# Attention chain on one core: head 0's k stack in halves, V projections between the scores, third reciprocal six steps earlier

## What is computed

```python
xn = group_norm(x) * gn_gamma + gn_beta
q, k, v = xn @ wq.T + bq, xn @ wk.T + bk, xn @ wv.T + bv     # 8 heads of 32
scores = einsum('bhqd,bhkd->bhqk', q * scale, k)
attn = softmax(scores, axis=-1)
o = einsum('bhqk,bhkd->bhqd', attn, v)
out = o @ wo.T + bo + residual
```

## Time and profile before

| what | value |
|---|---|
| median of 3 runs | 504.64 us (504.47 to 504.94) |
| the profiled execution's own time | 505.75 us |
| its span, first to last instruction | 504.0 us |
| mean granted TensorE clock | 0.971 of 2.4 GHz |
| busy: TensorE, weight loads | 474.6 us (94%), 241.0 us (48%) |
| busy: VectorE, ScalarE, GpSimd | 360.9 (72%), 270.2 (54%), 209.2 (42%) |

### The profile page before, as it was taken

The page is one execution under the profiler, slowest core; times in us unless marked ns, Lnnn a source line. Parts: engine busy times, 40 slices in busy tenths (PEclk is TensorE's granted clock), DMA queues, the critical chain, the costliest instruction groups (busy, mean ns, idle before and its releaser), DMA issues.

```text
span 504.0 us, 7046 instructions
## 1 busy us (share of the span) xinstructions
PE 474.6 (94%) x2252; PEld 241.0 (48%) x2252; DVE 360.9 (72%) x684; ACT 270.2 (54%) x518; POOL 209.2 (42%) x195
## 2 busy tenths in 40 slices
PE   8899999998999998999999999998899999999996
PEld 6454444443338664544444432664444444433363
DVE  6699888884853557987677747629798677748573
ACT  3238777776603323786667663131687566756032
POOL 8200021137010001799898951000589798990100
PEclk9979999999896998999999999999899999999999
DMA  5330432104100053387973541034257975352002
GB/s 148 59 59 17 139 66 36 21 13 85 23 12 1 13 128 89 66 193 153 183 174 67 99 91 23 1 87 109 66 113 155 185 149 101 58 98 48 17 2 83
DMA packets 19984, 40.69 MB, mean 81 GB/s; under 512 B 7282, under 2 KB 8442, under 8 KB 19820
## 3 DMA queue, kind: packets, MB, share of 16 engines
q1 hardware_dynamic: 14652, 24.23, 20.5%
q0 software_dynamic: 5152, 16.00, 17.2%
q10 hardware_dynamic: 144, 0.02, 0.0%
...
## 4 chain that ended last, share of the span: by engine, by line
PE 62%; issue 12%; DVE 7%; POOL 5%; SPq 4%; DMA 4%; ACT 4%; POOLq 0%; ACTq 0%; DVEq 0%
PE S L932 16%; PE S L959 12%; PE PV L970 10%; DVE max L696 5%; DMA k_stack<-kL 4%; PE S L1084 3%; PE PV L887 3%; POOL SUMS L489 3%; ACT E L552 3%; SPq L308 2%; PE M L913 2%; PE S L913 2%; PE PV L913 2%; PE S L1129 2%; SPq L315 1%
## 5 line engine op out<-in xcount | busy, mean ns | idle before, releaser
L696 DVE TENSOR_REDUCE max<-S 128x1 f32<-128x512 f32 x384 | 238.8, 674 | 19.2 <-PE S L932 18.8
L552 ACT ACTIVATE E<-S 128x512 f32<-128x512 f32 x384 | 211.9, 605 | 63.0 <-PE S L959 54.2
L489 POOL TENSOR_TENSOR SUMS<-E 128x512 f32<-128x512 f32 x120 | 158.2, 1437 | 125.4 <-ACT E L552 125.0
L932 PE MATMUL S<-k_stack,q_stack 126*128 126x512 f32 x384 | 181.2, 482 | 6.5 <-DVE max L696 3.2
L959 PE MATMUL S<-q_stack,k_stack 128*128 128x512 f32 x384 | 156.6, 420 | 9.1 <-ACT E L552 8.5
L932 PEld LDWEIGHTS S<-k_stack,q_stack 126*128 126x128 f32 x384 | 73.7, 192 | 82.4 <-DVE max L696 59.8
L959 PEld LDWEIGHTS S<-q_stack,k_stack 128*128 128x128 f32 x384 | 73.8, 194 | 38.5 <-ACT E L552 24.1
L970 PE MATMUL PV<-E,V 128*32 128x512 f32 x768 | 91.7, 598 | 0.0
L709 DVE TENSOR_TENSOR mHL<-S,mHL 4x128 fp32r<-4x128 f32 x48 | 13.3, 277 | 51.9 <-ACT mHL L541 51.9
L970 PEld LDWEIGHTS PV<-E,V 128*32 128x32 f32 x768 | 20.6, 109 | 46.6 <-issue 26.8
L468 POOL TENSOR_TENSOR att<-pv_sb,rec_sb 128x512 f32<-128x512 f32 x9 | 12.3, 1371 | 70.5 <-DMA rec_sb<-den_sb 70.5
(11 more groups left out here) (176 smaller groups left out, 339.2 us busy)
## 6 DMA issues: line engine op xcount, KB each, us to landing
...
k_stack<-kH SPq DMA_DIRECT2D x32, 128.0 KB, 2.4
q_stack<-qH SPq DMA_DIRECT2D x40, 64.0 KB, 2.0
...
k_stack<-kL SPq DMA_DIRECT2D x16, 128.0 KB, 3.7
q_stack<-qH SPq DMA_DIRECT2D x16, 128.0 KB, 2.3
q_stack<-mHL SPq DMA_DIRECT2D x96, 2.0 KB
q_stack<-qL SPq DMA_DIRECT2D x20, 64.0 KB, 2.0
```

The costliest lines, as they stand in the source:

```text
L489: pool.tensor_tensor(SUMS[:, slot, :], E[:, E_PLAN[s][0], :], E[:, E_PLAN[s + 1][0], :], ALU.add).then_inc(sum_ready, 1)
L552: act.activation(E[:, slot, :], B[:, ring_of_scores(s) % B_RING, :], ACT.Exp, scale=1.0 if l == 0 else float(HEAD_DIM[l]) ** -0.5).then_in ...
L696: dve.tensor_reduce(max8[:, m % 2, r:r + 1], A[:, n % A_RING, :], AX.X, ALU.max, negate=True).then_inc(a_used, 1)
L932: pe.matmul(A[:, n % A_RING, :], q_stack[0:SHIFT_ROW, slot, q0:q0 + P], k_stack[0:SHIFT_ROW, slot, k0:k0 + HALF], start=True, stop=True).t ...
```

## The change

Head 0's k stack is loaded in two halves of its columns, the first counting on `stack_dma[0]` and the second on a new semaphore, `half_dma`; the high parts of q and k are sent once ScalarE has written them, the low parts after the subtraction. The maxima of unit 0 take the first half of k for all four tiles of queries, then the second; the fifth score waits for `half_dma`. In layers 2 and 3 four projections instead of seven run ahead of the scores, the V projections between them at steps -15 to -1, and projections 8 to 11 at steps 1 to 15, with their copies and subtractions moved accordingly; ScalarE copies the last two V projections after the first rows of maxima. In all layers the third reciprocal moves from step 123 to 117, and GpSimd's normalisation waits for `pv_out` too.

```diff
--- before.py
+++ after.py
@@ -43,7 +43,7 @@
 RES = 16
 W_COLS = (3 * 128 + C, 4 * C, 4 * C)
 FOLDED = BLOCKS - 1
-REC_STEPS = (66, 94, 123)
+REC_STEPS = (66, 94, 117)
 PER_ROW = HALF // DP
 LEAD_GROWTH = (1, 3, 5, 7)
 VALUE_STEPS = ((29, 37, 45, 53), (61, 69, 77, 85), (93, 101, 107, 115))
@@ -189,6 +189,7 @@
         xn_ready = sem("xn_ready")
         proj_done, v_out, high_ready, split_ready = sem("proj_done"), sem("v_out"), sem("high_ready"), sem("split_ready")
         stack_dma = [sem(f"stack_dma{h}") for h in range(NH)]
+        half_dma = sem("half_dma")
         second_dma = [sem(f"second_dma{h}") for h in range(HEADS_B)]
         a_done, a_used = sem("a_done"), sem("a_used")
         negmax_ready, rows_done = sem("negmax_ready"), sem("rows_done")
@@ -231,11 +232,10 @@
         def v_count(l, n):
             return V0[l] + sum(x[0] == "v" for x in UNITS[l][:n + 1])
 
-        EARLY = (6, 7, 7)
-        LATE_PE = [{}] + 2 * [{-15: (7, 0), -13: (7, 1), -3: (8, 0), -1: (8, 1), 1: (9, 0), 3: (9, 1),
-                               5: (10, 0), 7: (10, 1), 9: (11, 0), 11: (11, 1)}]
-        LATE_ACT = [{}] + 2 * [{0: 8, 4: 9, 8: 10, 12: 11}]
-        LATE_DVE = [{}] + 2 * [{2: 8, 6: 9, 10: 10, 14: 11}]
+        EARLY = (6, 4, 4)
+        LATE_PE = [{}] + 2 * [{-15 + 2 * i: (4 + i // 2, i % 2) for i in range(16)}]
+        LATE_ACT = [{}] + 2 * [{5: 8, 9: 9, 13: 10, 17: 11}]
+        LATE_DVE = [{}] + 2 * [{7: 8, 11: 9, 15: 10, 19: 11}]
 
         def proj_bank(n):
             return (B[:, 0, :], B[:, 1, :], PV[:, :], M[:, :])[n] if n < 4 else (PV[:, :], M[:, :])[n % 2]
@@ -245,6 +245,13 @@
 
         def second_count(l):
             return 16 * 3 * (l + 1)
+
+        def half_count(l):
+            return 16 * 3 * (l + 1)
+
+        def maxima_tile(i):
+            r = i % TILES
+            return (r % 4, r // 4) if i < TILES else (r // 2, r % 2)
 
         def slot_of(h):
             return h % SLOTS
@@ -301,19 +308,23 @@
         def head_row(l, h):
             return 16 * h if l == 0 else DP * (h % 4)
 
-        def load_q(eng, l, h, cs, done):
+        first, second, both = slice(0, HALF), slice(HALF, N), slice(0, N)
+        HIGH_Q, LOW_Q = ((0, qH), (1, qH)), ((2, qL),)
+        HIGH_K, LOW_K = ((0, kH), (2, kH)), ((1, kL),)
+
+        def load_q(eng, l, h, cs, done, parts=HIGH_Q + LOW_Q):
 
             p, d, slot = head_row(l, h), HEAD_DIM[l], slot_of(h)
-            for blk, src in ((0, qH), (1, qH), (2, qL)):
+            for blk, src in parts:
                 eng.dma_start(q_stack[d * blk:d * (blk + 1), slot, cs].bitcast(F32),
                               src[p:p + d, cs].bitcast(F32)).then_inc(done, 16)
 
-        def load_k(eng, l, h):
+        def load_k(eng, l, h, cs, done, parts=HIGH_K + LOW_K):
 
             p, d, slot = head_row(l, h), HEAD_DIM[l], slot_of(h)
-            for blk, src in ((0, kH), (2, kH), (1, kL)):
-                eng.dma_start(k_stack[d * blk:d * (blk + 1), slot, :].bitcast(F32),
-                              src[p:p + d, :].bitcast(F32)).then_inc(stack_dma[h], 16)
+            for blk, src in parts:
+                eng.dma_start(k_stack[d * blk:d * (blk + 1), slot, cs].bitcast(F32),
+                              src[p:p + d, cs].bitcast(F32)).then_inc(done, 16)
 
         @block.sync
         def _(sp):
@@ -360,20 +371,24 @@
                              den_sb[0:P:DP, :].rearrange("u (o n) -> u o n", o=1)
                              .to_broadcast([HEADS_B, DP, HALF])).then_inc(recs_spread, 16)
 
-            first, second, both = slice(0, HALF), slice(HALF, N), slice(0, N)
             for l in range(LAYERS):
                 if l:
                     sp.wait_ge(b_done, STEPS * l)
+                sp.wait_ge(high_ready, QK0[l] + 1)
+                load_q(sp, l, 0, first, stack_dma[0], HIGH_Q)
                 sp.wait_ge(split_ready, QK0[l] + 1)
-                load_q(sp, l, 0, first, stack_dma[0])
-                sp.wait_ge(split_ready, QK0[l] + 3)
-                load_k(sp, l, 0)
+                load_q(sp, l, 0, first, stack_dma[0], LOW_Q)
+                for half, cs, done in ((0, first, stack_dma[0]), (1, second, half_dma)):
+                    sp.wait_ge(high_ready, QK0[l] + 2 + half)
+                    load_k(sp, l, 0, cs, done, HIGH_K)
+                    sp.wait_ge(split_ready, QK0[l] + 2 + half)
+                    load_k(sp, l, 0, cs, done, LOW_K)
                 for h in (1, 2):
                     load_q(sp, l, h, first, stack_dma[h])
-                    load_k(sp, l, h)
+                    load_k(sp, l, h, both, stack_dma[h])
                 shift_rows(l, 0)
                 load_q(sp, l, 3, first, stack_dma[3])
-                load_k(sp, l, 3)
+                load_k(sp, l, 3, both, stack_dma[3])
                 sp.wait_ge(split_ready, QK0[l] + 4)
                 for h in (0, 1):
                     load_q(sp, l, h, second, second_dma[h])
@@ -465,6 +480,7 @@
 
                 g, f = b // 2, b % 2
                 pool.wait_ge(recs_spread, 16 * (FOLDED * l + b + 1))
+                pool.wait_ge(pv_out, pv_count(l, b))
                 pool.tensor_tensor(att[:, g, HALF * f:HALF * (f + 1)], pv_sb[:, :], rec_sb[:, :],
                                    ALU.mult).then_inc(att_ready, 1)
 
@@ -521,6 +537,7 @@
                     return
                 high = (qH if kind == "q" else kH)[:, HALF * half:HALF * (half + 1)]
                 if c:
+                    act.wait_ge(half_dma, half_count(l))
                     for h in range(HEADS_B):
                         act.wait_ge(stack_dma[h], stack_count(l))
                         if kind == "q":
@@ -588,11 +605,13 @@
                     act.activation(gsmall[:, 4, :], M[:, 4:6], ACT.Sqrt,
                                    bias=eps[:, l:l + 1]).then_inc(sd_ready, 1)
                     act.activation(spare[:, 1:2], eps[:, 0:1], ACT.Exp).then_inc(eps_read, 1)
-                for n in range(8 if l else 6):
+                for n in range(6):
                     if l == 0 and n == 4:
                         act.wait_ge(v_ones, 1)
                     project_out(l, n)
                 high_rows(l, 0)
+                for n in range(6, 8 if l else 6):
+                    project_out(l, n)
                 for s in range(STEPS):
                     if s in ROWS_AT:
                         high_rows(l, ROWS_AT[s])
@@ -693,7 +712,8 @@
                 dve.wait_ge(a_done, n + 1)
                 if r == 0 and m >= 2:
                     dve.wait_ge(negmax_ready, m - 1)
-                dve.tensor_reduce(max8[:, m % 2, r:r + 1], A[:, n % A_RING, :], AX.X, ALU.max,
+                t, half = maxima_tile(i)
+                dve.tensor_reduce(max8[:, m % 2, 2 * t + half:2 * t + half + 1], A[:, n % A_RING, :], AX.X, ALU.max,
                                   negate=True).then_inc(a_used, 1)
                 if r == TILES - 1:
                     dve.wait_ge(a_used, n + 1)
@@ -926,9 +946,12 @@
                         pe.wait_ge(second_dma[h], second_count(l))
                     if l == 0 and h >= SLOTS:
                         pe.wait_ge(pos_late[h - SLOTS], 16 * POS_ROWS)
+                if i == HEADS_B:
+                    pe.wait_ge(half_dma, half_count(l))
                 if n >= A_RING:
                     pe.wait_ge(a_used, n - A_RING + 1)
-                q0, k0 = HALF * f + P * (r // 2), HALF * (r % 2)
+                t, half = maxima_tile(i)
+                q0, k0 = HALF * f + P * t, HALF * half
                 pe.matmul(A[:, n % A_RING, :], q_stack[0:SHIFT_ROW, slot, q0:q0 + P],
                           k_stack[0:SHIFT_ROW, slot, k0:k0 + HALF], start=True, stop=True).then_inc(a_done, 1)
```

## The result

| | before | changed kernel |
|---|---|---|
| median | 504.79 us (504.47 to 505.12, 4 runs) | 491.79 us (490.49 to 494.82, 4 runs) |
| ratio, 95% interval | | 0.9757 (0.9715 to 0.9799) |
| span of the profiled execution | 504.0 | 493.1 |
| granted TensorE clock | 0.971 | 0.975 |

Forecast were 488.3 us (485.0 to 495.5): 16.3 us saved. Measured are 13.0. The four runs of the changed kernel were 494.82 (the profiled one), 490.7, 492.89 and 490.49: a scatter of 4.3 us. The kernel before had 0.65 in its four runs here, but 3.9 to 4.8 in the ten or eleven of the later comparisons, so the scatter isn't the change's own. A second set of four runs gave 490.39 (489.64 to 491.82) against 504.18 for the kernel before beside it, and that profile is the better one to compare with; where the two differ is the story of the experiments. Layers 2 and 3 are the second and third attention layer.

A forecast was written before the change was run, and what follows sets the result against it. TensorE was taken as 62% of the chain, with the gain at attention layers' starts and ends. Terms 13.2 + 0.4 + 2.7 = 16.3 us saved took the median from 504.64 to 488.3 us, range 485.0 to 495.5.

The forecast's parts named there:

- Part 1, first score: Start of layers 2 and 3: with head 0's k in halves, the first score for maxima starts 3.9 us earlier.
- The fit that the prediction quoted from that page: Transfer time as 2.0 us plus bytes by 436 GB/s; by it a half lands 0.15 us sooner than a whole.
- Steps -16 to 0: Layers 2 and 3, first score to step 0: TensorE and VectorE level, 1.34 us per pair, 11.0 us in all.
- Steps 0 to 29: Layers 2 and 3: ScalarE's 2.69 us hole goes; stretches to steps 8, 16 and 29 take 8.6, 7.6 and 8.7 us.
- Part 2: Layer 1's start: halves remove the first score's 0.71 us wait; gain between 0 and 0.8, taken as 0.4 us.
- Part 3: End of all layers: earlier third reciprocal removes the output projection's 0.90 us wait for GpSimd; 2.7 us, bounds 0 and 2.8.
- The forecast's own range: Whole kernel: 18.8 down to 12.4 us saved, that is 485.8 to 492.2 us.
- A: Rival: TensorE's clock falls at the start of layers 2 and 3, costing 2.2 us per layer: 492.7; chance 0.14.
- B: Rival: transfers crowd; k's first half and loads for steps 5 and 13 late, 2.6 us a layer: 493.5; chance 0.09.
- C: Rival: the third reciprocal waits for its input at step 117, holding up the last additions: 491.0; chance 0.05.
- D: Rival: slower, TensorE bound from step -16 to 16 with the clock staying down, up to 515.5; chance 0.06.
- E: Rival: a later bound swallows the start's gain, leaving parts 2 and 3: 501.5, with C 504.2; chance 0.05.

The follow-up runs named there:

- whole_k: Changed kernel with head 0's k stack in one piece after the third subtraction and unit 0's maxima in the old order: 498.19 us, ratio 0.9867.
- act_q1: spread_later with layer 1's k whole and old order of maxima, plus ScalarE issuing head 1's q in layers 2 and 3: 493.16 us, ratio 0.9766.
- l1_whole: Changed kernel with head 0's k halves and the new order of maxima only in layers 2 and 3: 490.94 us, ratio 0.9757.
- rec123: Changed kernel with the third reciprocal back at step 123 instead of 117: 493.38 us, ratio 0.9792.
- spread_later: Changed kernel with the second block's reciprocal spread behind unit 14's shift rows instead of unit 13's: 493.34 us, ratio 0.9782; again 495.02, 0.9831.
- late_only: Kernel before with only the second projections, their copies and subtractions later in layers 2 and 3: 501.94 us, ratio 0.996.
- after_again: The changed kernel unaltered, measured a second time against the kernel before: 490.39 us, ratio 0.9732.

## Why the prediction was right, and where it was not

**Part 1, first score: right.** Forecast 8.2 after the first projection, measured 8.01. SP's issues came where they were worked out: first shift rows 16.1 after the first projection (184.96), the second unit's 25.0 (193.85). TensorE's idle time was 0.87 instead of 1.2. The Trainium skill's advice in "DMA: Bandwidth & Descriptors", "Rules for kernel authors", is to coalesce many small transfers, with the overhead put below 64 KB; a half of kL is just 64 KB. `whole_k` measures what k in one piece costs here: a first score 2.55 later. What decides is that a piece can be issued before the rest exists. The fit that the prediction quoted from that page is stated for transfers issued from GpSimd, and these are SP's; nothing in the sum rested on it.

**Steps -16 to 0: 0.8 too short** (11.0 forecast, 11.8 measured). The pace of 1.34 per pair holds (178.13 to 180.80 for two pairs, 1.33 each). The step that failed is the one on SP's queue: "heads 1 and 2 at 186.3 (twelve issues of 0.63)" was used for the shift rows only, and not for head 1's kL, the sixth of them. It is issued at 180.51 and lands 2.4 later, and the ninth score, due at 182.47, waits for it until 182.93. An earlier first score moves the need for head 1 as well, and there SP's three extra issues are not hidden. `act_q1` gives the 0.7 back.

**Steps 0 to 29: right within 0.3** (8.6, 7.6 and 8.7 forecast; 8.3, 7.8 and 8.9 measured). ScalarE doesn't wait at step 5, the clock is 1.00 from 168 to 216. Together a layer saves 5.9 and 6.1 to step 29 instead of 6.6: 12.0 of 13.2. The term was mis-sized at the ninth score, inside its bounds.

**Part 2: wrong sign, too small to tell.** The first score is 0.94 earlier, from 21.02 to 20.08, but there head 1's kL is waited for too, 1.06 at 25.29. SP's three extra issues then push the second unit's shift rows from 36.87 to 37.22, and step 8 waits 0.71 instead of 0.22. "It gains only about 0.1" was the step that failed: step 8 is 0.35 later (39.23 to 39.58), and the fourteen traces put the loss at 0.4. `l1_whole` shows that this is within the noise of the times.

**Part 3: right**, in size (3 x 0.9) and mechanism, by the profile and by `rec123`, whose 3.0 us fit the 2.7, though its profile has the wait in two layers only.

**The range.** The forecast's own range goes down to 12.4 us saved with 2.4 for part 3, but that part's own lower bound is 0. With it the range ends at 10.0 saved, 494.6 us, still inside 485.0 to 495.5. The measured 13.0 lie inside both, near the low end. That they do has luck in it: the order at step 111 and the layer norm's clock shift single executions by some 4 and 1.4 us, and the forecast had neither.

**The rivals.** A did not come: some 0.87 us of idle time left the clock up in all 22 traced layers that have it. That it was a real one is shown by `whole_k`'s third layer. B came in part, at one of the three places that it named: qL for step 13, in some layers of some executions, 1 to 1.9 us each. C did not come here, but in `spread_later`. D did not come. E came in a small part: from step 61 to 69 part of a layer's gain goes again (below), 0.6 in layer 2 of the first profile, 1.1 and 0.5 in layers 2 and 3 of the second.

**What the forecast did not have.** The profiled execution lost 4.5 us in one layer, 0.6 of it before step 69 and 4.0 at step 111, the latter by the order of two issues 0.07 us apart. The earlier trace rows showed that transfers slow each other, and I looked for it only at the layer's start. The pair was in the trace of before as well, the sums at 282.03 and the broadcast at 282.12 with 8.4 to landing, and TensorE's denominators had room for that. For this pair the profile before shows only this order, but the other order, with 10.7 and 11.3 to landing, stood in it at the first block's broadcast, where TensorE did not wait for the sums. Two more terms are smaller. From step 61 to 69 TensorE waits for head 7's kL, 0.88 in the first profile's layer 2 and 1.41 and 1.13 in the second's layers, 0.32 and 0.60 in the kernel before. I tried nothing on that, so its cause is argued: the load starts with its step, and meets sums that are issued at other distances than before. `late_only` has it too (0.92 and 1.13), so it doesn't need the halves. And the layer norm ahead of layer 2, from output projection to the next layer's first projection, takes 26.4 to 27.8 in the three profiles where it took 29.44, of which 0.9 is part 3. Clock there, the kernel before, the changed kernel's profile, then `after_again` (columns as above):

```profile
154.00:166.00 12.00, 11.40 (x62) 11.32 (x62) 4.98 (x9) 3.64 (x6) 0.00 (x0) 0.57 0.01 1
```

```profile
155.00:165.00 10.00, 8.86 (x53) 8.59 (x52) 5.26 (x10) 3.42 (x5) 0.00 (x0) 0.68 0.01 2
```

```profile
154.00:164.00 10.00, 8.46 (x62) 8.18 (x61) 5.40 (x11) 3.32 (x5) 0.00 (x0) 0.83 0.01 2
```

These are 10.3, 6.4 and 3.4 us at the lower level of 1.2 GHz. Most of that is not a gain of the change: `late_only`, whose first layer and reciprocals are those of the kernel before, takes 27.97 there, 1.5 less than the one profile of before. So up to 1.5 us of the distance between the two profiled executions is the moment's.

**The scatter.** Traces show two places where the time depends on which of two transfers is issued first: step 13 (up to 1.9 us a layer) and step 111 (some 4). In the changed kernel's three profiles each occurred once in six layers. Two more depend on the clock: the spell near step 120 (1.5 to 1.6, in six of 28 layers, none of them the changed kernel's) and the layer norm ahead of layer 2 (up to 3 us between traces, of which part 3 is 0.9). The span of the profiled run of 494.82 is 4.2 above that of `after_again`: 3.4 more from step 29 to the output projection of layer 2, 1.4 more in the layer norm, 0.6 less in layer 3. For the runs without a trace which of these they had stays open, and for the kernel before, with its one trace, all of it.
